# A two-block adaLN layer on one core: unrolled, four batches in flight, and the token shift through ScalarE and PSUM

## The reference

```
h  = layernorm(x) * (1 + ca) + sa
u, gate = split(h @ W_in.T)
b  = u @ W_state.T ;  dt = min(softplus(u @ W_dt.T + b_dt), 10)
decay = exp(-dt * rate)
state[t] = decay[t] * state[t-1] + (1 - decay[t]) * b[t]
z  = (state @ W_C.T) * silu(gate) + h * D
x1 = x + ga * (z @ W_out.T)
h2 = layernorm(x1) * (1 + cb) + sb ;  h2p = h2 one token earlier (0 at the first)
xr = mu_r * h2 + (1 - mu_r) * h2p ;  xk = mu_k * h2 + (1 - mu_k) * h2p
out = x1 + gb * sigmoid(xr @ W_r.T) * (relu(xk @ W_k.T)^2 @ W_v.T)
```

## Time and profile before

| | us |
|---|---|
| median of 3 runs | 406.45 (406.3 to 408.54) |
| profiled execution, its time | 406.4 |
| its span | 404.6 |
| first scan starts | 20.0 |
| last scan starts | 363.4 |
| one batch later, in the middle (L357 at 206.40 and 229.12) | 22.7 |

### The profile page before, as it was taken

The page is one execution under the profiler, slowest core; times in us unless marked ns, Lnnn a source line. Parts: engine busy times, 40 slices in busy tenths (PEclk is TensorE's granted clock), DMA queues, the critical chain, the costliest instruction groups (busy, mean ns, idle before and its releaser), DMA issues.

```text
span 404.6 us, 5464 instructions
## 1 busy us (share of the span) xinstructions
PE 378.3 (93%) x1616; PEld 264.0 (65%) x1619; DVE 349.3 (86%) x675; ACT 290.9 (72%) x355; POOL 229.0 (57%) x206
## 2 busy tenths in 40 slices
PE   7885899999999999999999999999999999999875
PEld 4562657676776767676776767676766767676532
DVE  3788697989999898999999898999999898959692
ACT  4673269787878869687878869687878869694633
POOL 2124177474848577474848477474848576564700
PEclk9988799999999999999999999999999999999999
DMA  8810110040402204040402104040403112010102
GB/s 299 319 54 0 58 67 34 0 159 0 156 0 76 81 7 148 0 156 0 156 0 85 71 20 136 0 156 0 156 0 95 62 40 65 0 53 0 52 2 104
DMA packets 18590, 28.97 MB, mean 72 GB/s; under 512 B 1168, under 2 KB 9616, under 8 KB 18448
## 3 DMA queue, kind: packets, MB, share of 16 engines
q1 hardware_dynamic: 18144, 28.71, 20.7%
q10 hardware_dynamic: 432, 0.09, 0.1%
HBM read 20.40 MB, written 8.39 MB: 71 GB/s over the span
## 4 chain that ended last, share of the span: by engine, by line
PE 48%; DVE 42%; issue 5%; ACT 2%; DMA 1%; POOL 0%; POOLq 0%; DVEq 0%; ACTq 0%; SPq 0%
PE slot L256 35%; DVE xr L693 8%; PE slot L357 7%; DVE z L725 5%; DVE slot L720 5%; DVE h_diff L675 5%; DVE x L689 4%; DVE xk L693 4%; DVE slot L681 4%; PE slot L326 4%; DVE stats L565 1%; DMA w_in<-weights_in 1%; DVE gate_abs L647 1%; PE slot L417 1%; DVE xn L586 1%
## 5 line engine op out<-in xcount | busy, mean ns | idle before, releaser
L796 POOL TENSOR_TENSOR xk_lo<-xk,xk_hi 128x512 fp32r<-128x512 f32 x30 | 51.3, 1729 | 26.5 <-ACT xk_hi L468 26.5
L417 PE MATMUL slot<-z,w_in 128*128 128x512 f32 x128 | 57.6, 592 | 0.0
L828 POOL TENSOR_TENSOR h_diff<-h 128x512 f32<-128x512 f32 x15 | 18.9, 1258 | 56.8 <-ACT h L514 56.8
L461 ACT ACTIVATE h<-slot,mod 128x512 f32<-128x512 f32 x32 | 24.7, 777 | 25.8 <-PE slot L295 25.8
L796 POOL TENSOR_TENSOR h_lo<-h,h_hi 128x512 fp32r<-128x512 f32 x30 | 38.2, 1298 | 7.6 <-ACT h_hi L468 7.6
L256 PE MATMUL slot<-h_hi,wf_hi 128*128 128x512 f32 x128 | 40.4, 418 | 1.5 <-ACT h_hi L468 1.5
L295 PEld LDWEIGHTS slot<-ident,xn 128*128 128x128 f32 x256 | 27.7, 141 | 21.5 <-DVE xn L586 11.7
L789 POOL TENSOR_TENSOR rstd<-mv,eps 128x4 f32<-128x4 f32 x32 | 7.4, 233 | 58.9 <-DVE mv L582 58.9
L295 PE MATMUL slot<-ident,xn 128*128 128x128 f32 x256 | 34.2, 276 | 5.3 <-DVE z L725 3.5
L256 PE MATMUL slot<-h_hi,wf_lo 128*128 128x512 f32 x128 | 38.6, 403 | 0.0
L417 PEld LDWEIGHTS slot<-z,w_in 128*128 128x128 f32 x128 | 23.3, 190 | 23.3 <-issue 23.0
(11 more groups left out here) (105 smaller groups left out, 919.8 us busy)
## 6 DMA issues: line engine op xcount, KB each, us to landing
x_tok<-x_tok_in SPq DMA_DIRECT2D x16, 512.0 KB, 4.4
x_ch<-x_ch_in SPq DMA_DIRECT2D x16, 512.0 KB, 5.1
x_out<-x SPq DMA_DIRECT2D x15, 512.0 KB, 3.2
wmod<-wmod_in SPq DMA_DIRECT2D x1, 1024.0 KB, 8.2
w_in<-weights_in SPq DMA_DIRECT2D x1, 1024.0 KB, 10.9
w_in<-weights_in SPq DMA_DIRECT2D x1, 768.0 KB, 5.5
wmod<-wmod_in SPq DMA_DIRECT2D x1, 512.0 KB, 6.5
x_out<-x SPq DMA_DIRECT2D x2, 256.0 KB, 2.0
```

Of the source, the lines that this page charges most:

```text
L417: last = nc.tensor.matmul(ps_o[:, d, :], w_late[:, c, OUT + d * P:OUT + (d + 1) * P], z[:, c, :], start=(c == 0), stop=(c == CH - 1))
L461: last = nc.scalar.activation(h[:, q, c, :], ps[:, c, :], ACT.Identity, bias=mod_at(c, k), scale=mod_at(2 + c, k))
L796: nc.gpsimd.tensor_tensor(lo, x, hi.bitcast(F32), ALU.subtract).then_inc(done, 1)
```

## The change

The kernel is rewritten. What it does differently:

- **Unrolled.** The hardware loop goes; a Python loop over steps s = 0 to 19 writes all instructions out. In step s, batch a = s is loaded and normed, b = s-1 is in its first block, c = s-2 in the second norm and the token shift, d = s-3 in the key, receptance and value products. `xn1`'s statistics, mean and 1/std have two buffers, `x_tok` and `x1` three, `x2` two (in the memory of `wmod`).
- **Pieces of products.** `half` issues one pass of one input half. The passes of the products of four batches are interleaved by hand, so that each low part is asked for late.
- **The output product** z @ W_out in three passes, with `z_hi` on ScalarE and `z_lo` on GpSimd (12 matmuls of fp32r in place of 4 of float32 per batch). All of the late weights are split, in four pieces.
- **The token shift.** `h2` and `h2_diff` go. ScalarE reads the transposed norm from PSUM four times per batch and writes `prev` (scale times (1 - mu), plus shift), one column on; VectorE's mix reads the same PSUM and `prev`: xk = ps_n * (scale * mu) + prev. GpSimd sets the first column. The tables for that come from 10 more small operations on VectorE at the start.
- **Smaller ones.** 1/std takes eps in `mean_variance`, which saves a GpSimd operation per norm. The two ScalarE operations on the gate go: r * v becomes (tanh + 1) * v, and x2 takes the gate in its own operation. `ln1_mean_variance` stands behind r * v, apart from its statistics. The last batches take the three-pass products too.

The diff, cut to its core:

```diff
-            def split_product(outs, w_hi, w_lo, at, x_hi, x_lo, hi_ok=None, lo_ok=None, count=0, lo_halves=range(CH)):
-
-
-                passes(outs, w_hi, at, x_hi, start=True, there=hi_ok, count=count)
-                passes(outs, w_lo, at, x_hi)
-                return passes(outs, w_hi, at, x_lo, halves=lo_halves, stop=True, there=lo_ok, count=count)
+
+            for s in STEPS:
+                a, b, c, d = s, s - 1, s - 2, s - 3
+                if live(d):
+                    if d == 0:
+                        pe.wait_ge(wl_lo_ok, 4)
+                    pe.wait_ge(xkhi_ok[0], d + 1)
+                    for x_done in (*xk_ok, *xr_ok):
+                        pe.wait_ge(x_done, d + 1)
+                    half(k_out, wl_hi, MIX_K, xk_hi, 0, first=True)
+                    half(k_out, wl_lo, MIX_K, xk_hi, 0)
+                if live(c):
+                    pe.wait_ge(zlo_ok[0], c + 1)
+                    half(o_out, wl_hi, OUT, z_lo, 0)
+                if live(d):
+                    pe.wait_ge(xkhi_ok[1], d + 1)
+                    half(k_out, wl_hi, MIX_K, xk_hi, 1)
+                    half(k_out, wl_lo, MIX_K, xk_hi, 1)
+                if live(c):
+                    pe.wait_ge(zlo_ok[1], c + 1)
+                    half(o_out, wl_hi, OUT, z_lo, 1, last=True).then_inc(o_ps, 1)
...
+                if live(c):
+                    pe.wait_ge(x1_ok[0], c + 1)
+                    pe.wait_ge(x1_ok[1], c + 1)
+                    for t in range(TT):
+                        for i in range(CH):
+                            last = nc.tensor.transpose(ps_x1[:, t, i * P:(i + 1) * P], x1[:, c % 3, i, t * P:(t + 1) * P], ident[:])
+                    last.then_inc(t2_ps, 1)
+                if live(d):
+                    pe.wait_ge(xrhi_ok[0], d + 1)
+                    if not live(c):
+                        pe.wait_ge(tanh_ok, d)
+                    half(r_out, wl_hi, MIX_R, xr_hi, 0, first=True)
+                    half(r_out, wl_lo, MIX_R, xr_hi, 0)
+                if live(b):
...
+                        pe.wait_ge(s_wy, 16)
+                    pe.wait_ge(state_ok, b + 1)
+                    for i in range(CH):
+                        last = nc.tensor.matmul(ps_y[:, i, :], w_y[:, i * P:(i + 1) * P], state[:], start=True, stop=True)
+                    last.then_inc(y_ps, 1)
...
-            schedule(pe, iteration)
+                    pe.wait_ge(zhi_ok[0], b + 1)
+                    before(pe, tanh_ok, d + 1 if live(d) else 0)
+                    half(o_out, wl_hi, OUT, z_hi, 0, first=True)
+                    half(o_out, wl_lo, OUT, z_hi, 0)
+                if live(d):
+                    pe.wait_ge(klo_ok[1], d + 1)
+                    half(v_out, wl_hi, MIX_V, k_lo, 1, last=True).then_inc(v_ps, 1)
+                if live(b):
+                    pe.wait_ge(zhi_ok[1], b + 1)
+                    half(o_out, wl_hi, OUT, z_hi, 1)
+                    half(o_out, wl_lo, OUT, z_hi, 1)
...
+            def previous(mix, i, k):
+                return nc.scalar.activation(prev[:, mix, i, 1:T + 1], ps_n[:, i, :], ACT.Identity,
+                                            bias=mod_at(SHIFT2 + i, k), scale=mix_prev[:, mix, i, k:k + 1])
+
+            for s in STEPS:
+                a, b, c, d = s, s - 1, s - 2, s - 3
+                if live(c):
+                    act.wait_ge(z_ok[1], c + 1)
+                    nc.scalar.copy(z_hi[:, 1], z[:, 1]).then_inc(zhi_ok[1], 1)
...
+                if live(c):
+                    if c == 0:
+                        act.wait_ge(mix_ok, 1)
+                    act.wait_ge(t3_ps, c + 1)
+                    before(act, xk_ok[0], c)
+                    previous(KEY, 0, c)
+                    before(act, xr_ok[0], c)
+                    previous(REC, 0, c).then_inc(prev_ok[0], 1)
+                if live(b):
+                    act.wait_ge(z_ok[0], b + 1)
+                    before(act, o_ps, b)
+                    nc.scalar.copy(z_hi[:, 0], z[:, 0]).then_inc(zhi_ok[0], 1)
+                if live(c):
+                    before(act, xr_ok[1], c)
+                    previous(REC, 1, c)
+                    before(act, xk_ok[1], c)
+                    previous(KEY, 1, c).then_inc(prev_ok[1], 1)
...
-                before(dve, st_ok, k + 1)
+                dve.wait_ge(st_ok, k + 1)
                 nc.vector.tensor_tensor(mv[:, 2, :], st[:, :, 1], st[:, :, 4], ALU.subtract)
-                nc.vector.tensor_tensor(mv[:, 3, :], st[:, :, 2], st[:, :, 5], ALU.add).then_inc(halves_ok, 1)
-                before(dve, halves_ok, k + 1)
+                nc.vector.scalar_tensor_tensor(mv[:, 3, :], st[:, :, 2], EPS * C, st[:, :, 5], ALU.add, ALU.add).then_inc(halves_ok, 1)
...
+            def mixed(x, mix, i, k, done):
+
+                nc.vector.scalar_tensor_tensor(x[:, i, :], ps_n[:, i, :], mix_now[:, mix, i, k:k + 1], prev[:, mix, i, 0:T], ALU.mult, ALU.add).then_inc(done, 1)
...
-            def difference(c, done):
-
-                nc.vector.tensor_tensor(h2_diff[:, c], h2[:, c, 1:T + 1], h2[:, c, 0:T], ALU.subtract).then_inc(done, 1)
...
-            def mix(out, mu, c):
-
-                return nc.vector.scalar_tensor_tensor(out[:, c, :], h2_diff[:, c, :], col(mu + c), h2[:, c, 0:T], ALU.mult, ALU.add)
...
-                    before(dve, diff_ok[0], k)
-                    before(dve, xkhi_ok[1], k - 1)
-                    before(dve, xklo_ok[1], k - 1)
-                    mix(xk, MU_K, 0).then_inc(xk_ok[0], 1)
-                    before(dve, diff_ok[1], k)
-                    mix(xk, MU_K, 1).then_inc(xk_ok[1], 1)
-                    before(dve, xrhi_ok, k - 1)
-                    before(dve, xrlo_ok[1], k - 1)
-                    mix(xr, MU_R, 0)
-                    mix(xr, MU_R, 1).then_inc(xr_ok, 1)
-                    if tail:
-                        gated_v(k)
-                        second_residual(m, r)
...
+                if live(c):
+                    dve.wait_ge(first_ok, c + 1)
+                    dve.wait_ge(prev_ok[0], c + 1)
+                    before(dve, xklo_ok[0], c)
+                    mixed(xk, KEY, 0, c, xk_ok[0])
+                    before(dve, xrlo_ok[0], c)
+                    mixed(xr, REC, 0, c, xr_ok[0])
+                    dve.wait_ge(prev_ok[1], c + 1)
+                    before(dve, xrlo_ok[1], c)
+                    mixed(xr, REC, 1, c, xr_ok[1])
+                    before(dve, xklo_ok[1], c)
+                    mixed(xk, KEY, 1, c, xk_ok[1])
+                if live(a + 2) and a > 0:
+                    ln1_stats(a + 2)
+                if live(d):
+                    dve.wait_ge(v_ps, d + 1)
+                    dve.wait_ge(tanh_ok, d + 1)
+                    nc.vector.scalar_tensor_tensor(ps_v[:], r_gate[:], 1.0, ps_v[:], ALU.add, ALU.mult).then_inc(rv_ok, 1)
+                if live(a + 2) and a > 0:
+                    ln1_mean_variance(a + 2)
+                if live(d):
+                    dve.wait_ge(rv_ok, d + 1)
+                    before(dve, s_out[d % 2], 16 * (d // 2))
+                    for i in range(CH):
+                        nc.vector.scalar_tensor_tensor(x2[:, d % 2, i], ps_v[:, i], mod_at(GATE2 + i, d), x1[:, d % 3, i, :], ALU.mult, ALU.add).then_inc(x2_ok[i], 1)
+                if live(b):
+                    dve.wait_ge(o_ps, b + 1)
+                    dve.wait_ge(s_xc[b % 2], 16 * (b // 2 + 1))
+                    for i in (1, 0):
+                        before(dve, x2_ok[i], b - 2)
+                        nc.vector.scalar_tensor_tensor(x1[:, b % 3, i, :], ps_o[:, i, :], mod_at(GATE1 + i, b), x_ch[:, b % 2, i, :], ALU.mult, ALU.add).then_inc(x1_ok[i], 1)
...
+                if live(a):
+                    dve.wait_ge(e_ok, a + 1)
+                    nc.vector.tensor_scalar(dt[:], dt[:], EXP_MAX, None, ALU.min).then_inc(clip_ok, 1)
...
+                    dve.wait_ge(t2_ps, b + 1)
+                    statistics(ps_x1, stats2[:, b % 2], st2_ok)
+                    before(dve, rstd2_ok, b - 1)
+                    mean_variance(stats2[:, b % 2], mv2[:, b % 2], st2_ok, halves2_ok, spread2_ok, mv2_ok, b)
...
+            for s in STEPS:
+                a, b, c, d = s, s - 1, s - 2, s - 3
+                if live(d):
+                    for i in range(CH):
+                        low_part(xk_lo[:, i], xk[:, i], xk_hi[:, i], xkhi_ok[i], k_ps, xklo_ok[i], d)
+                if live(b) and b > 0:
+                    for i in range(CH):
+                        low_part(h_lo[:, i], h[:, b % 2, i], h_hi[:, i], hhi_ok, g_ps, hlo_ok[i], b)
+                if live(d):
+                    low_part(xr_lo[:, 0], xr[:, 0], xr_hi[:, 0], xrhi_ok[0], r_ps, xrlo_ok[0], d)
+                if live(c):
+                    pool.wait_ge(mv2_ok, c + 1)
+                    before(pool, xn2a_ok, c - 1)
+                    before(pool, xn2b_ok, c - 1)
```

(27 more changed lines are left out.)

778 lines of the change are left out of this document (315 added, 463 removed).

## The result

The changed kernel takes 419.1 us (median of four, 416.6 to 425.2) against 406.5: ratio 1.028 [1.025, 1.032]. The forecast was 406, no change within 1%; it became slower, though still inside the range of 380 to 420.

What follows compares the result with a forecast made beforehand. It took a chain of waits, one loop of 22.7 us per batch through VectorE and TensorE, as the bound. Start 21.2 + 24.2 + 18.9, 11 x 23.4, 2 x 21.2 and tail 40.1 gave 404.2, plus 1.8: 406.0 us, range 380 to 420.

Steps and rivals of the forecast that it cites:

- group one waits to 12.2, group two to 13.4, group three to 14.7: Middle steps, VectorE: first norm's mean and variance waits three times for GpSimd's low parts, 3.1 us instead of 0.7.
- TensorE waits 2.1: Middle steps: TensorE could transpose x1 at 15.3 but x1 ends at 17.4, making the step 23.4 us.
- those with two SBUF inputs meet GpSimd's weight splits: Step 1, table operations on VectorE: waits up to 1.28 us each, in all about 3.
- Tail: From the last scan's end to the end of the kernel: 40.1 us, with 2.5 after the last x2.
- the wait in front of x1: Middle steps: a wait before x1 replaces the old loop's behind x2; 23.4 us per step against 22.7.
- the floor: TensorE's own work per batch in the middle, the least a step can take: 21.1 us.
- z's price: VectorE mixes with one input in PSUM: taken at 0.745 us like z, bounds 0.65 and 1.2.
- the passes at 0.233: TensorE: one pass of a three-pass matmul takes 0.233 us, kept from the trace over the skill's 0.213.
- Rival C: Middle steps: `mv1` arrives one GpSimd operation later, for example through slower mixes; 24.7 us per step, 420 us; 22%.
- A: The forecast case: three waits of `mv1` cancel the gain, 406 us, 399 to 413 alone; 50%.
- Rival B: Middle steps: `mv1` meets a GpSimd gap after one short wait, TensorE sets the pace; 382 us; 28%.

Runs made afterwards that it cites:

- the run with zeros: Changed kernel plus six bf16 matmuls of zeros on TensorE before its wait for x1: 423.3 us, ratio 1.032.
- `mv1` behind the clip: Changed kernel with the first norm's mean and variance (`mv1`) moved behind the clip, after the work TensorE waits for: 392.1 us, ratio 0.963.
- the run with three of them: `mv1` behind the clip, plus three chained one-SBUF-input TENSOR_SCALAR on 128x32 in `mv1`'s old place: 411.6 us, ratio 1.010.

## Why the prediction was wrong

- **The step that failed: "group one waits to 12.2, group two to 13.4, group three to 14.7", 3.1 us.** It took `mv1` as three groups with one wait each. It is five operations, and the second of a pair can lose its place as well. In five of eleven steps it did: 4.5 us, 1.4 more per step (24.6 against 23.2 in the run with zeros). The earlier trace rows held only the case in which the second of a pair slips through. With three waits in all eleven steps the same execution would have taken 12.8 less, 412, so this step, with the clock behind it, is the larger part of the 19 us and not all of it.
- **A term that was missing: TensorE's clock.** "TensorE waits 2.1" was priced as time. After an idle time of 3.1 it mostly comes back at 1.2 GHz; four of the five steps read 0.93. Eleven steps at 23.2 would be 255.2; they took 268.0. Five fourth waits at 1.4 are 7.0 of the 12.8; the 5.8 left lie in the four steps whose clock fell and those behind them, by subtraction.
- **Start: "those with two SBUF inputs meet GpSimd's weight splits", about 3.** Seven operations at 1.2 in place of 0.18 are 7.1 us, five of them with one SBUF input. On VectorE's path that is 4.1 more than forecast, of the 4.9 by which step 1 is longer. The clock has a share as well: with these seven waits and the tables in this place step 1 took 27.2 at a mean clock of 0.81 (`mv1` behind the clip) and 30.4 at 0.66 (the changed kernel once more), and the y product in it 1.96 in the first of these and 3.76 in the second, where 1.73 was forecast. The runs do not part the two. The earlier trace rows had no small operation with one SBUF input beside GpSimd; the statistics are another kind. The Trainium skill, SBUF — State Buffer, Who interferes with whom, says that `tensor_scalar` can take the shared pair as well when it enters a two-port mode; by that rule the tables wait, and the trace and the run with three of them (1211 ns) agree.
- **Tail: 1.8 short.** Counted from the last scan's end (381.2) the last x2 ends 1.1 later than walked (419.9), and the end comes 3.2 behind it in place of 2.5. Plain float32 in the last batch takes 1.2 to 2.0 off; the tail of the versions with three passes and the shift through PSUM is 41.9 to 43.4.
- **Right:** the wait in front of x1 in place of the one behind x2, its walk (23.2 measured, 23.4 forecast in a step with three waits), the floor (21.4 against 21.2), the mixes at z's price, the passes at 0.233.
- **Rival C** had the size (24.7 per step, 420 us) by the wrong cause: the mixes cost 0.746 and `mv1` arrived when forecast, 11.3 after y for 11.5. That 419.1 lies beside its 420, and inside the range, is luck. (Its chances also leave a little out: a fifth, three fifths and a sixth of A are 29 thirtieths of it.) **Rival B**'s mechanism, `mv1` in a gap, is what `mv1` behind the clip makes by hand: 392 against its 382; the 10 are a start 4.8, a tail 2.6 and eleven steps 2.7 longer than its sum, less 0.3 in the last two steps.
